# Causal heads of a two-layer gated cross-attention block: another order of groups, copies and waits

## The reference, cut to what matters

```
r = x + tanh(g_xattn[0]) * cross_attention_16_heads(LN(x), ctx)           # "l0"
r = r + tanh(g_ffn[0]) * bitlinear_ffn(LN(r))                             # "f0": int8-like rounding
x1 = LN(r); q, k, v = LN(x1) @ wq, LN(x1) @ wk, LN(x1) @ wv               # "a1": 16 heads of width 32
a = softmax(q k^T * 32**-0.5)                                             # 512 x 512 per head
a = a * (t > s)                                                           # mask AFTER the softmax: keys behind the query
x1 = x1 + concat(a v) @ li1 ; x1 = x1 + gelu(LN(x1) @ li2) @ li3          # then "a2" (cross), "f1" (one expert)

_act_quant(x): scale = 127 / clip(max|x|, 1e-5); xq = clip(round(x * scale), -128, 127) / scale
```

## Time and profile before

| | us |
|---|---|
| median of 3 runs | 426.03 (424.16 to 428.45) |
| the profiled execution's own time | 422.04 |
| its span, first to last instruction | 420.3 |
| mean granted TensorE clock | 0.943 of 2.4 GHz |
| head loop, 138.2 to 280.4 | 142.2 |

### The profile page before, as it was taken

One profiled execution on the slowest core, in us unless ns is written; L12 is line 12 of the kernel. 1 busy time (PEld: TensorE's weight loads), 2 busy tenths in 40 slices (PEclk: granted clock), 3 DMA queues, 4 the chain that ended last, 5 costly groups with the idle time before them and its releaser, 6 DMA issues.

```text
span 420.3 us, 6805 instructions
## 1 busy us (share of the span) xinstructions
PE 344.0 (82%) x2037; PEld 235.8 (56%) x2038; DVE 315.2 (75%) x748; ACT 279.4 (66%) x965; POOL 107.6 (26%) x206
## 2 busy tenths in 40 slices
PE   4978999726437888998989988978998799977796
PEld 4756877602312444555545545566676588864656
DVE  3656789688885688899899998975757876855515
ACT  4465888657413787888889888853825899855051
POOL 5311344300010122232222222232101444520100
PEclk9999999966558999999999999999999899999989
DMA  7920000000003653861790494000000000000001
GB/s 222 346 100 2 2 1 2 1 0 1 2 0 82 158 136 89 200 140 26 168 207 3 101 205 96 0 4 0 2 0 2 1 2 0 2 0 2 0 0 51
DMA packets 8860, 24.75 MB, mean 59 GB/s; under 512 B 2667, under 2 KB 2744, under 8 KB 8568
## 3 DMA queue, kind: packets, MB, share of 16 engines
q1 hardware_dynamic: 8824, 24.32, 22.9%
HBM read 7.00 MB, written 0.52 MB: 18 GB/s over the span
## 4 chain that ended last, share of the span: by engine, by line
PE 43%; DVE 13%; issue 7%; ACT 7%; POOL 1%; DVEq 0%
PE ps L397 9%; PE ps L537 5%; PE ps L521 5%; DVE nm L1513 4%; PE ps L615 4%; PE ps L667 4%; PE ps L490 4%; PE ps L630 4%; ACT pring L1111 3%; PE ps L470 3%; PE ps L438 2%; DVE arena L1485 2%; PE ps L701 2%; DVE xn L1182 1%; PE ps L683 1%
## 5 line engine op out<-in xcount | busy, mean ns | idle before, releaser
L1111 ACT ACTIVATE pring<-ps,nm 128x512 f32<-128x512 f32 x128 | 87.0, 688 | 12.7 <-DVE nm L1513 9.6
L988 ACT ACTIVATE arena<-ps,nmx 128x77 f32<-128x77 f32 x256 | 79.1, 344 | 14.1 <-DVE nmx L1248 13.6
L1513 DVE TENSOR_REDUCE nm<-ps 128x2 f32<-128x1024 f32 x64 | 78.0, 1220 | 6.1 <-PE ps L630 5.9
L875 POOL TENSOR_SCALAR_AFFINE_SELECT pring<-pring 128x128 f32<-128x128 f32 x128 | 38.8, 303 | 109.5 <-ACT pring L1111 109.5
L630 PE MATMUL ps<-Ks,Qs 128*128 128x512 f32 x128 | 52.6, 463 | 8.6 <-ACT pring L1111 6.2
L397 PEld LDWEIGHTS ps<-ident,pring 128*128 128x128 f32 x352 | 39.4, 140 | 32.7 <-issue 17.8
L397 PE MATMUL ps<-ident,pring 128*128 128x128 f32 x352 | 52.1, 277 | 6.7 <-ACT xn L1078 2.8
L988 ACT ACTIVATION_READ_ACCUMULATOR arena<-ps,nmx 128x1 f32 x256 | 57.3, 224 | 0.0
L851 POOL TENSOR_TENSOR arena<-arena,rden 128x616 f32<-128x616 f32 x32 | 39.2, 1226 | 63.1 <-DVE rden L1253 63.1
L490 PE MATMUL ps<-arena 128*128 128x128 f32 x320 | 42.4, 280 | 6.3 <-DVE arena L1260 6.3
L490 PEld LDWEIGHTS ps<-arena 128*128 128x128 f32 x320 | 38.6, 192 | 15.5 <-DVE arena L1260 14.9
(11 more groups left out here) (147 smaller groups left out, 539.4 us busy)
## 6 DMA issues: line engine op xcount, KB each, us to landing
Qs<-qh SPq DMA_DIRECT2D x24, 128.0 KB, 2.4
Qs<-ql SPq DMA_DIRECT2D x24, 128.0 KB, 2.4
Ks<-xo SPq DMA_DIRECT2D x24, 128.0 KB, 2.4
Ks<-xb SPq DMA_DIRECT2D x24, 128.0 KB, 2.4
wa_sb<-in_wa SPq DMA_DIRECT2D x1, 1536.0 KB, 15.2
early<-in_w SPq DMA_DIRECT2D x2, 512.0 KB, 8.2
wa_sb<-in_wa SPq DMA_DIRECT2D x1, 1024.0 KB, 17.4
Qs<-hid SPq DMA_DIRECT2D x16, 64.0 KB, 2.0
```

What stands on the lines that cost most here:

```text
L875: pool.affine_select(out=blk, in_=blk, compare_op=ALU.is_gt, fill=0.0, base=0, pattern=[[1, P]], channel_multiplier=-1).then_inc(masked, 1)
L988: ins = act.activation(Pc[:, i % PC_SLOTS, h * HS:h * HS + M], bank(where[key])[:, h % 4 * HS:h % 4 * HS + M], ACT.Exp, bias=nmx[:, i % 4, ...
L1111: release(act.activation(pring[:, n % 2, i, :], bank(f"S{i}"), ACT.Exp, bias=nm1[:, n % 8, i:i + 1], accum_out=den1[:, n % 8, i:i + 1]), ( ...
L1513: dve.tensor_reduce(nm1[:, n % 8, 2 * u:2 * u + 2], pair(u), AX.X, ALU.max, negate=True).then_inc(nm1_ready, 1)
```

## The change

- Groups run batch by batch: `group k` is batch `k // 4`. The four products ahead of the loop are those of batch 0 alone (groups 0 and 1). Batch 1 is normalised, transposed and evacuated inside the loop (n = 0, 2, 4), its values are made at n = 9 to 12 in bank B, which the projections use as well.
- Piece 2 has three blocks instead of four; DVE copies it for even heads' weights (at odd n), ACT for odd ones (at even n, between the exponentials of blocks 1 and 2). All blocks stand in compact slots, 8 of them instead of 6, and key block 3's own diagonal block becomes a 32-column matmul of width 128 of its own.
- On PE the inverse sums' transposes and the values of key blocks 3 and 2 stand at n mod 4 = 2 between piece 1 and `scores(n, 2)`; those of 1, 0 and the diagonal block at n mod 4 = 3 in the same place. Projection and late values stand at the end of the iteration.
- On ACT `high_half` stands at the end of iteration n, behind the exponentials; on DVE `low_half` stands at the end, behind both reductions and ahead of head n+1's.
- The broadcast copy of the inverse sums goes from DVE to POOL.
- f0's two clips go, and the factors 127 and 1/127 are folded into neighbouring instructions.

```diff
-        PIECES = [[(0, 0), (0, 1), (0, 2), (0, 3)], [(1, 1), (1, 2), (1, 3)], [(2, 2), (3, 2), (2, 3), (3, 3)]]
-        LATE_VALUES = [0, 1, 6, 8]
+        PIECES = [[(0, 0), (0, 1), (0, 2), (0, 3)], [(1, 1), (1, 2), (1, 3)], [(2, 2), (2, 3), (3, 3)]]
...
+        def group(k):
+
+            return k // NG, k % NG
+
+        def value_tile(n):
+
+            return NT + n - 9 if 9 <= n < 9 + NT else None
...
-            for n in range(NHB + 3):
-                k = (n - 1) // HG - 1
+            for n in range(NHB + 2):
                 if n < NHB:
                     scores(n, 0)
-                if n in LATE_VALUES:
-                    project_values(NT + LATE_VALUES.index(n), "B" if n else "A")
-                if next_projection(n):
-                    project(next_projection(n))
+                    scores(n, 1)
                 if 1 <= n <= NHB:
                     p_transposes(n - 1, 0)
                     p_transposes(n - 1, 1)
+                if 6 <= n < NHB and n % HG == 2:
+                    sums_transposes(n // HG - 1)
+                    values(n // HG - 1, (3, 2))
+                if 6 <= n < NHB and n % HG == 3:
+                    values(n // HG - 1, (1, 0))
                 if n < NHB:
-                    scores(n, 1)
-                if n >= HG and n % HG == 1:
-                    values(k, (3,))
-                if n >= HG and n % HG == 2:
-                    values(k, (1, 0))
+                    scores(n, 2)
+                    scores(n, 3)
                 if 1 <= n <= NHB:
                     p_transposes(n - 1, 2)
+                if n == NHB + 1:
+                    sums_transposes(NGRP - 1)
+                    values(NGRP - 1, (3, 2, 1, 0))
+                if next_projection(n):
+                    project(next_projection(n))
+                if n == 4:
+                    ln_transposes("a1", 1)
+                if value_tile(n):
+                    project_values(value_tile(n), "B")
                 if n == NHB:
                     li1(0)
-                if n >= HG and n % HG == 1:
-                    values(k, (2,))
-                if n >= HG and n % HG == 2:
-                    sums_transposes(k)
...
-            for n in range(NHB + 4):
-                if next_projection(n):
-                    high_half(next_projection(n))
+            for n in range(NHB + 2):
                 if 1 <= n <= NHB:
-                    key = ("p1", n - 1, 0)
+                    pt_copy(n - 1, 0)
                 for u in range(2):
...
+                    if u == 0 and 1 <= n <= NHB and n % 2 == 0:
+                        pt_copy(n - 1, 2)
-                if n > HG and n % HG == 2:
+                if 6 <= n < NHB and n % HG == 2:
                     sums_across(n // HG - 1)
+                if next_projection(n):
+                    high_half(next_projection(n))
+                if n == 4:
+                    a1_evac(1)
+                if value_tile(n) and value_tile(n) % 2 == 0:
+                    copy_values(value_tile(n))
...
+            for m in range(4):
+                low_half(m)
+            copy_values(1)
+            copy_values(3)
             ln_stats("ln1", 1, r)
             ln_norm("ln1", 1, r, ("ln1_g", "ln1_b"), x1)
...
-                    if u == 1 and next_projection(n):
-                        low_half(next_projection(n))
-                    if 1 <= n <= NHB:
+                    if u == 0 and HG <= n <= NHB and n % HG == 0:
+                        inverse_sums(n // HG - 1)
+                    if 1 <= n <= NHB and (u == 0 or n % 2):
                         pt_copy(n - 1, 1 + u)
+                if next_projection(n):
+                    low_half(next_projection(n))
+                if value_tile(n) and value_tile(n) % 2:
+                    copy_values(value_tile(n))
+                if n == 0:
+                    ln_stats("a1", 1, x1)
+                if n == 2:
+                    ln_norm("a1", 1, x1)
+                if 6 <= n < NHB and n % HG == 3:
+                    normalise(n // HG - 1)
...
+                if n % HG == HG - 1:
+
+                    k = n // HG
+                    pool.wait_ge(rd1_ready, k + 1)
+                    if k:
+                        pool.wait_ge(RT_ready, k)
+                    pool.tensor_copy(rdx[:, :, :, :], rd1[:, :, :].rearrange("p h t -> p t h").unsqueeze(3)
+                                     .to_broadcast([P, NT, HG, D1])).then_inc(rdx_ready, 1)
...
-                if 2 <= n < NB * NT + 2:
-                    j = n - 2
-                    dve.wait_ge(hround_ready, j + 1)
-                    dve.tensor_scalar(h_in[:, j % 4, :], h_in[:, j % 4, :], MAGIC + 127.0, MAGIC - 128.0,
-                                      ALU.min, ALU.max).then_inc(hclip_ready, 1)
```

More of the change, by code:

```diff
@@ L139, in build @@
         cols_sb = sb("cols_sb", [P, NCOL])
-        halves = {k: sb(k, [P, NB, TOK], F32R) for k in ("qh", "ql")}
+        halves = {k: sb(k, [P, 2, TOK], F32R) for k in ("qh", "ql")}
         for k, place in (("kh", xo), ("kl", xb)):
@@ L605, in project @@
             def project(m):
-                which, b, g = projection(m)
+                which, e, q = projection(m)
+                b, g = group(2 * q + e)
                 if which == "q":
@@ L615, in project, with scores @@
                 filled(pe.matmul(bank(res), w[:, g * P:(g + 1) * P], src[:, b, :], start=True, stop=True), ("qk", m))
-            def scores(n, u):
-                k, b, g, j = head(n)
-                if u == 0:
+            def scores(n, i):
+                e, j = n // HG % 2, n % HG
+                claim(pe, f"S{i}", ("s1", n, i), read_by=(exp1_done, NT * n + i + 1))
+                if i == 0:
                     if n < EARLY:
                         pe.wait_ge(first_stack[n], 16 * 8)
[L624 to L631, removed]
+                    elif n % (2 * HG) < HG or HG <= n < HG + EARLY:
+                        pe.wait_ge(stack_q[j], 16 * 4 * (n // (2 * HG) + 1))
+                        pe.wait_ge(stack_k[j], 16 * 4 * (n // (2 * HG) + 1))
+                filled(pe.matmul(bank(f"S{i}"), Qs[:, j, e, i * P:(i + 1) * P], Ks[:, j, e, :],
+                                 start=True, stop=True), ("s1", n, i))
             turn = [0]
@@ L1067, in high_half @@
             def high_half(m):
-                which, b, g = projection(m)
+                which, e, q = projection(m)
                 halves_free(act, m)
                 res = await_bank(act, ("qk", m))
-                act.activation(part(which + "h", g)[:, b, :], bank(res), ACT.Copy,
+                act.activation(part(which + "h", q)[:, e, :], bank(res), ACT.Copy,
                                scale=float(D1) ** -0.5 if which == "q" else 1.0).then_inc(hi_ready, 1)
             def sums_across(k):
+                if k:
+                    act.wait_ge(OT_ready, k)
                 res = await_bank(act, ("rt", k))
@@ L1277, in cross @@
                         scale_x(0)
-                    if site == "l0" and i == NU + 1:
-                        clip_x(0)
                     if site == "a2" and i == 0:
@@ L1433, in _ @@
                     scale_x(1)
-                if n == 1:
-                    clip_x(1)
                 if n == NB * NT:
@@ L1450, in low_half @@
                 res = await_bank(dve, ("qk", m))
[L1451 to L1452 removed]
+                ins = dve.scalar_tensor_tensor(part(which + "l", q)[:, e, :], bank(res), scale,
+                                               part(which + "h", q)[:, e, :].bitcast(F32), ALU.mult, ALU.subtract)
                 release(ins, ("qk", m))
@@ L1532, in _ @@
                     ln_stats("a1f", 0, xo)
-                if n > HG and n % HG == 3:
-                    normalise(n // HG - 1)
+                if n == NHB + 1:
+                    normalise(NGRP - 1)
             ln_norm("a1f", 0, xo)
```

229 lines of the change are left out of this document (107 added, 122 removed).

## The result

The changed kernel takes 464.79 us (median of 4 runs, 461.21 to 467.42) against 425.1 (422.21 to 428.45) for the one before in the same session: ratio 1.0925, interval 1.0799 to 1.1051. Forecast was 454.0, so the sign was right and the size 10.8 too small. The profiled execution took 467.42 us itself, with a span of 465.7; its forecast was 449.7.

What follows compares the result with a forecast made beforehand. No engine was full: program order in a ring through PE, DVE and ACT bounds the loop, DVE f0. Span 420.3 + 33.5 (`li1` later) - 0.7 (tail) - 5.1 (f0) = 448.0; execution 449.7, median 453.7, say 454; range 436 to 471.

Steps and rivals of the forecast that it cites:

- Projection heads: Loop, 12 of 32 heads: low half waits behind all exponentials, so 5.44 us between first reductions against 4.62.
- Group work: Loop, n mod 4 = 2 and 3, seven times: transposes and values delay scores; four plain heads 19.15 or 17.75 us, before 16.34.
- Late values: Loop, n = 10 to 12: bank B makes PE wait for low halves, 1.8 us each, 5.4, plus 0.3 for a copy.
- The clock: Loop matmuls priced at the full clock, since idle pieces there are under 3 us; a fall was left to a rival.
- Start: Up to head 0: batch 1's ln1 moves behind low halves; first reduction 139.1 instead of 140.24, about 134 with f0's 5.1.
- f0 as a whole: f0 without clips and with factors folded in: 5.1 us less in all, 4 to 6 by what bounds it.
- the term of a unit: f0, DVE's row: clip and x127 step gone, 0.52 us less in each of five units, 2.6.
- Tail: Behind `li1`: inverse sums' transposes ahead of the last values and RT ready earlier, 0.7 us less.
- The load decides: Rival: engines' busy work sets the time, so the lighter DVE makes it faster, 411 us; chance 0.07.
- Only the projection chain costs: Rival: group work hides; projection heads, late values and batch 1's part cost, 437 us; chance 0.13.
- The clock's rival: Rival: PE's clock falls to 1.2 GHz in the loop, 460 to 480 us, taken as 470; chance 0.18.
- the likeliest case: The time as forecast, 454 us, with its own range 446 to 462; chance 0.60.

Runs made afterwards that it cites:

- e1: Changed kernel with projections, high halves and low halves back in their places from before the change: 452.13 us, 1.0675 of the kernel before.
- e2: Changed kernel with values and inverse sums' transposes behind scores 2 and 3 again, as before the change: 442.59 us, 1.045 of the kernel before.
- e3: Changed kernel with batch 1's late values at heads 6 to 9 instead of 9 to 12: 455.18 us, 1.0758 of the kernel before.
- e5: Changed kernel with the edits of e1, e2 and e3 together: 420.7 us, 0.9981 of the kernel before.
- e7: Changed kernel plus two unread 512-column matmuls on PE ahead of piece 0 at n mod 4 = 3: 465.27 us, 1.1015 of the kernel before.
- e9: e5 with the inverse sums' transposes of groups 0, 2, 4, 5, 6 in bank B: 423.04 us, 0.9998 of the kernel before.
- e4: Kernel before the change with only f0's edits (both clips out, factors folded in): 417.97 us, 0.9877 of the kernel before.
- e8: e5 with batch 1's ln1 on DVE ahead of the first low half, as before the change: 422.93 us, 0.9999 of the kernel before.
- e10: e5 with the copy of piece 2 on DVE for every head: 418.79 us, 0.9895 of the kernel before.
- e11: Kernel before with f0's edits (e4) and the inverse sums' transposes of groups 2, 4, 5, 6 in bank B: 417.14 us, 0.985 of the kernel before.
- e12: e5 with the edits of e9 and e10 together: 421.83 us, 0.9957 of the kernel before.

## Why the prediction was right, and where it was short

*The mechanism.* All waits named for the profile after are there: low halves 1.5 to 2.5 us late, transposes behind piece 0's copy, piece 0 behind RT, values in bank B behind low halves. e1, e2 and e3 show that they are the loss: 10.6, 20.2 and 7.1 us alone, and 40.1 when all three go (e5).

*Projection heads.* Right: 5.55 and 5.42 (265.46 to 270.88) for the 5.44 worked out; the block 25.80 for 25.75, with 8.66, 6.17, 5.55 and 5.42 for its four heads where 8.5, 6.05, 5.75 and 5.45 had been worked out; 10.6 (with its 5 of error) for 9.8 as a whole.

*Group work.* 17.75 and 17.85 forecast for heads 14 to 17 and 6 to 9. At full clock with two idle products added it was 17.98 and 18.10 (e7). Heads 26 to 29 of the changed kernel itself, at 1.00, took 19.50 (290.63 to 310.13) for 19.15. Right at that clock; as the kernel runs, 1.8 and 1.4 short.

*Late values.* Mis-sized: 5.7 forecast, 10.4 measured (e3's block against after's). The forecast took 0.86 and 0.84 for matmuls and about 1.8 in all for each; the wait before the value at 199.02 alone was 3.47, and value and scores then ran at the lower clock, 2.05 and 1.84 in duration: 3.00 from there to DVE's reduction (202.02), where the ones at 210.02, behind a wait of 2.98, took 1.67 at the higher clock.

*The clock.* This is the step that failed. The sum took matmuls at 2.4 GHz, on the argument that no idle piece in the loop is over 3 us, and the clock stood as a rival of its own at 470. It was neither: part of each row of the table but one. The argument was false twice. The change itself made longer waits, up to 3.47 us ahead of late values; and in four heads of five the clock also fell in waits of 2.65 us for RT, which the prediction had, but priced at the full clock. In heads 7, 15, 23 and 31 that cost 6.05 of the 14.3 us by which the loop ran over, and at the late value of 199.02 another 1.33 (3.00 for 1.67). For the rest there is only an estimate: in heads 0 to 29 the changed kernel has 720 records of PE in 124.1 us, 0.172 each, e5 has 736 in 113.3, 0.154 each, so that the same matmuls ran some 736 x 0.018 = 13 us longer than in e5 (itself at 0.89 in heads 0 to 5). Not all of it need stand in the ring; the blocks ran 12.2 over in those heads. The four executions of the changed kernel point the same way: two with a mean granted clock of 0.921 took 461.21 and 462.27 us, two with 0.914 took 467.31 and 467.42.

*Start.* First reduction 136.55 where 134.0 was forecast. In the nine kernels among the experiments that have the same program up to there it came between 134.12 (e7) and 136.13 (e9), 134.16 in e5; so the forecast was met by some executions, and this one was late. Its `l0` ended 0.8 later than before (84.90 for 84.11). f0 as a whole gave 5.2 for 5.1 (e4, with 2 either way), though the term of a unit was too large: 0.41 instead of 0.52, 2.0 instead of 2.6 for five, so the close sum is in part luck. How the normalisation acts was misread. It stands right in front of the first reduction, and with it put back (e8) that reduction came 3.4 us earlier, but the transfers for head 1 then took the gain.

*Tail.* `li1` to the end took 465.7 - 325.75 = 139.95, before 420.3 - 280.31 = 139.99: nothing in place of -0.7.

*The sum.* Start +2.5, loop +14.3, tail +0.7 make 17.5, and the execution is 467.42 for 449.7, +17.7. The median is only 10.8 over, because 4.0 had been added for the place of the profiled execution of before, while the one of after lay 2.6 above its own median.

*Rivals.* "The load decides" falls twice: by the waits, and by e5 and e10, where a lighter DVE gave no time and a heavier one took none. "Only the projection chain costs" (437) falls by e2. The clock's rival named the right effect, but at 470 it counted it too high as a case of its own. The range of the likeliest case, 446 to 462, was too narrow by the clock's part; 436 to 471 held.

*Open.* Whether e11's bank is worth anything over e4 once the transfers keep up, and how the clock's price is spread over the start and the blocks with projections. Neither a kernel with bank B spared at n = 6 nor one with fewer or earlier transfers was tried. Why the clock stayed up in head 27, behind the same wait, no run shows.

## What to carry to other kernels

In a ring through several engines, list for each moved instruction what waits behind it in its own program, and price it by that; the engines' busy times did not tell it here, and work taken off an engine that only waited came back as waiting. A bank is part of the program order: in this kernel whoever shares one waits for the last user's reader, and everything behind it on PE waits too. A faster stretch can meet a limit that was hidden before, here SP's transfers at heads 1 and 18. When a change adds waits of PE like those of 2.65 to 3.47 us here, price the matmuls at both clock levels, and read experiments by block, since one total can hide a gain and a loss.

## What the runs showed of the hardware

The broadcast copy of 512 columns took POOL 0.61 us, where 0.8 had been put between 0.30 and 1.2 (in e5; L918). Behind a wait of PE of 2.65 us, the same in length and in the work around it, the granted clock went to its lower level in heads 7, 15, 23 and 31 and stayed at 1.00 in head 27; after 2.98 us (210.02) it was up, after 3.47 us (199.02) down. So the length of the single wait does not tell the cases apart, and no run isolated what does. The same chain of matmuls took 2.73 us at 1.00 and 3.95 to 4.50 us with the lower level in it. ACT's high half at head 18 waited for a transfer out of `ql` 1.84 us in e5, 2.41 in e9, 2.61 in e11 and 3.00 in e12, and for none in the kernel before.
